# A two-layer FFN kernel on one core: the second layer's transposes move from TensorE to VectorE

## The reference

```python
def _L1_cond_ref(x, c, weight, c_weight, bias):
    out = lax.conv_general_dilated(x, weight, window_strides=(1,), padding=[(4, 4)],
                                   dimension_numbers=('NCH', 'OIH', 'NCH'), feature_group_count=4)
    return out + (c @ c_weight.T)[:, :, None] + bias[None, :, None]

def _L1_ffn_ref(x, up, down, perm):            # H = 16 heads, d = 128, m = 512
    t = x.reshape(-1, 2048)[:, perm].reshape(-1, 16, 128)
    t = gelu(einsum('bhd,hdm->bhm', t, up), approximate=False)
    t = einsum('bhm,hmd->bhd', t, down).reshape(-1, 2048)
    return t[:, argsort(perm)]
x = x + _L1_ffn_ref(_L1_cond_ref(x, cond_128, ...), up, down, perm)
```

## Time and profile before

| | |
|---|---|
| time, median of 3 runs | 2580.77 us (2577.89 to 2582.27) |
| the profiled execution's own time | 2583.87 us |
| its span (first to last instruction) | 2582.0 us |
| TensorE busy | 2528.0 us, 98% |
| VectorE busy | 1822.8 us, 71% |
| ScalarE busy | 1001.8 us, 39% |
| GpSimd busy | 950.8 us, 37% |
| moved by DMA | 541.02 MB, mean 210 GB/s |
| mean granted TensorE clock | 0.996 of 2.4 GHz |

### The profile page before, as it was taken

One profiled execution on the slowest core, in us unless ns is written; L12 is line 12 of the kernel. 1 busy time (PEld: TensorE's weight loads), 2 busy tenths in 40 slices (PEclk: granted clock), 3 DMA queues, 4 the chain that ended last, 5 costly groups with the idle time before them and its releaser, 6 DMA issues.

```text
span 2582.0 us, 39106 instructions
## 1 busy us (share of the span) xinstructions
PE 2528.0 (98%) x12090; PEld 2099.3 (81%) x12090; DVE 1822.8 (71%) x2667; ACT 1001.8 (39%) x1632; POOL 950.8 (37%) x826
## 2 busy tenths in 40 slices
PE   8899999999999999999999999999999999999997
PEld 6788888888888888888888778888888888888775
DVE  6665555965556755576445768888888888888876
ACT  3221212321122322232222555555555555555573
POOL 2366645466654455233223212222222222222231
PEclk9999999999999999999999999999999999999998
DMA  9965644665545777576555754577767676777786
GB/s 318 322 196 199 201 168 155 238 210 197 196 163 185 228 229 228 161 250 210 160 165 186 223 153 131 170 219 219 221 214 226 205 223 205 225 226 223 212 281 240
DMA packets 417281, 541.02 MB, mean 210 GB/s; under 512 B 36248, under 2 KB 270064, under 8 KB 417072
## 3 DMA queue, kind: packets, MB, share of 16 engines
q1 hardware_dynamic: 314816, 307.40, 39.6%
q10 hardware_dynamic: 78144, 154.27, 15.9%
q0 software_dynamic: 24112, 76.80, 9.4%
HBM read 309.72 MB, written 228.61 MB: 208 GB/s over the span
## 4 chain that ended last, share of the span: by engine, by line
PE 91%; DVE 4%; DMA 2%; issue 2%; ACT 1%; ACTq 0%; SPq 0%; POOL 0%; DVEq 0%; POOLq 0%
PE ps_c L461 44%; PE ps_up L1398 13%; PE ps_y L1408 13%; PE ps_c L1423 9%; PE ps_v L439 4%; PE ps_c L427 2%; PE ps_zt L1436 2%; PE ps_f L1444 2%; DVE w_lo L1004 1%; PE ps_up L1423 1%; DVE ring_lo L951 0%; DVE r_early L1000 0%; DMA a_s<-in_lora_a 0%; DMA x_n<-in_up 0%; DMA aggw_d<-agg 0%
## 5 line engine op out<-in xcount | busy, mean ns | idle before, releaser
L461 PE MATMUL ps_c<-w_hi,ring_hi 128*128 128x512 f32 x1792 | 703.8, 393 | 3.8 <-DVE r_early L1000 3.2
L461 PE MATMUL ps_c<-w_hi,ring_lo 128*128 128x512 f32 x1792 | 698.0, 390 | 0.0
L461 PE MATMUL ps_c<-w_lo,ring_hi 128*128 128x512 f32 x1792 | 697.8, 389 | 0.0
L611 ACT ACTIVATE ring_hi<-raw_n 128x512 fp32r<-128x512 f32 x382 | 239.4, 631 | 848.7 <-DVE raw_n L942 235.1
L1380 POOL DMA_INDIRECT y_d<-y_s,idx x128 | 145.7, 1139 | 723.1 <-ACT y_s L1548 689.6
L1505 ACT ACTIVATE kern<-ps_up 128x512 f32<-128x512 f32 x512 | 306.6, 599 | 257.5 <-PE ps_up L1398 245.4
L461 PEld LDWEIGHTS ps_c<-w_hi,ring_hi 128*128 128x128 f32 x1792 | 336.7, 188 | 74.5 <-issue 4.0
L461 PEld LDWEIGHTS ps_c<-w_hi,ring_lo 128*128 128x128 f32 x1792 | 336.4, 188 | 70.2
L461 PEld LDWEIGHTS ps_c<-w_lo,ring_hi 128*128 128x128 f32 x1792 | 336.7, 188 | 67.3
L1622 DVE TENSOR_TENSOR g_lo<-kern,g_hi 128x512 fp32r<-128x512 f32 x512 | 354.5, 692 | 38.2 <-ACT g_hi L1509 21.8
L1000 DVE TENSOR_TENSOR r_early<-ps_c,r_early 128x512 f32<-128x512 f32 x256 | 176.6, 690 | 276.2 <-PE ps_c L461 276.2
(11 more groups left out here) (211 smaller groups left out, 3832.9 us busy)
## 6 DMA issues: line engine op xcount, KB each, us to landing
u_d<-raw_n ACTq DMA_DIRECT2D x64, 512.0 KB, 3.2
x_d<-r_early ACTq DMA_DIRECT2D x128, 256.0 KB, 3.6
raw_n<-u_d SPq DMA_DIRECT2D x64, 512.0 KB, 3.6
x_d<-x_s ACTq DMA_DIRECT2D x126, 256.0 KB, 2.7
u_s<-x_d SPq DMA_DIRECT2D x496, 64.0 KB, 2.2
z_d<-x_s SPq DMA_DIRECT2D x120, 256.0 KB
rear<-y_d SPq DMA_DIRECT2D x112, 256.0 KB
rear<-x_d SPq DMA_DIRECT2D x112, 256.0 KB, 4.0
```

Source lines behind the costliest of these rows:

```text
L461: mm = nc.tensor.matmul(bank, a[:, dc, :], w[k][:, dc, :], start=(first and dc == 0 and n == 0), stop=(dc == 3 and n == 2), skip_group_che ...
L611: nc.scalar.activation(ring_hi[g % RING][:].rearrange("p a n -> p (a n)"), factor(q, k, p), ACT.Copy).then_inc(hi_ready, 1)
```

## The change

TensorE's `turn_z` and `turn_y`, with their banks `ps_zt` and `ps_f`, go. VectorE transposes 32x32 blocks inside each quarter of the partitions instead: `turn_z` from `z_s` straight into `zt` (in place of `take_z`), and, for two steps at once, `turn_y` from the loaded rows into `o_s`, followed one step later by `add_x1`, without a stride. For that the layouts change: a tile `zt` holds one group of four batches, a store of it takes one quarter of the partitions (32) with 16 pieces of 512 bytes each, rows of `y_d` come back in four DMAs of 32 partitions, the residual and the output move 512 KB for a pair of steps in 1 KB pieces, and `out` is written phase by phase and reordered on the host. There are two `z_s`, two pairs `t_hi`/`t_lo` (split two steps ahead, gathered three ahead), and two result banks `ps_y`. ScalarE makes two of four high parts of the hidden layer in all steps. A second pair of split convolution inputs for the lead steps has its own memory, and waits for layer 0's end go with that. A tile's store is issued in the step of its last convolution, no longer two steps later.

```diff
-                    sh.load_group(sp, x1_d, sh.xp[t - 4], t - 4, 0, t - 4)
+                    sh.load_group(sp, x1_d, sh.xp[t - 4], t - 4, t - 4, 0)
...
-        ps_c, ps_zt, ps_y, ps_f = bank("ps_c"), bank("ps_zt"), bank("ps_y"), bank("ps_f")
+        ps_c, ps_last = bank("ps_c"), bank("ps_last")
+        ps_y = [bank(f"ps_y{j}") for j in range(2)]
...
+        def by_scalar(mc):
+            return mc % 2 == 0
...
+        def final_part(dram, k, w):
+            first, cols = SB * (k - 1), slice(w % 2 * 2 * P, (w % 2 + 1) * 2 * P)
+            return dram[bass.ds(first, SB), :, w // 2, cols].rearrange("b c q -> c b q")
+        def z_rows(dram, r, part):
+            return dram.rearrange("(w i r) n -> r i w n", w=WIDE, r=S)[r, :, :, part * C:(part + 1) * C]
...
-            def load_final(k, h, parity):
+            def load_rows(k, h, parity):
...
-                wait(sp, fin_done, v - 1)
-                sp.dma_start(yt_s[j], y_d[1 - parity][c * 512:(c + 1) * 512, h // 4 * C:(h // 4 + 1) * C]
-                             .rearrange("(l p) r -> p l r", p=P)).then_inc(yt_in[j], 16)
-                wait(sp, o_ready, v - 1)
-                sp.dma_start(x1_s[j], x1_d[b, :, :, c * P:(c + 1) * P]).then_inc(x1_in[j], 16)
+                wait(sp, fin_done, pair(k, h))
+                rows = y_d[1 - parity].rearrange("(q w i s) n -> q s i w n", q=2, w=8, s=S)[w % 2, w // 2]
+                for g in range(G):
+                    sp.dma_start(yt_s[g * GC:(g + 1) * GC, :].rearrange("p (w n) -> p w n", w=8),
+                                 rows[:, :, g * C:(g + 1) * C]).then_inc(yt_in, 16)
+            def load_final_x1(k, h):
+                wait(sp, o_out, 16 * pair(k, h))
+                sp.dma_start(x1_s.rearrange("p (b q) -> p b q", b=SB), final_part(x1_d, k, h // 2)).then_inc(x1_in, 16)
...
+                for r in range(2 if isinstance(u, int) and u == H - 1 else S):
+                    sp.dma_start(z_rows(z_d[(parity + ahead) % 2], r, jb),
+                                 zt_of(k, h)[r * GC:(r + 1) * GC].rearrange("p w b c -> p w (b c)")).then_inc(z_out[jb % 2], 16)
...   (SyncE's step)
+                if h % 2 == 0 and pair_exists(k, h):
+                    load_rows(k, h, parity)
+                if h % 2 == 1 and pair_exists(k, h):
+                    load_final_x1(k, h)
+                if exists(k, h, LEAD) and (h + LEAD) % G == G - 1:
+                    store_z(k, h, parity)
+                if h % 2 == 0 and pair_exists(k, h, 1):
+                    store_out(*before(k, h, 2))
...   (TensorE)
-                if exists(k, h, LEAD - 1):
-                    turn_z(*before(k, h))
-                if final_exists(k, h, 1):
-                    turn_y(*before(k, h))
...
-                    wait(pe, y_ready, s)
+                    wait(pe, y_ready, s - 1)
...   (ScalarE)
-                    wait(act, zt_done, u - 1 if paired(k, h) else u)
+                    wait(act, zt_ready, u - 1)
+                    nc.scalar.activation(z_s[h % 2][:], conv_bank(k, h), ACT.Identity,
...   (VectorE)
+            def turn_z(k, h):
+                dve.wait_ge(z_ready, u + 1)
...
+                nc.vector.transpose(zt_of(k, h)[:, :, n % SB, :], z_s[h % 2][:]
+                                    .rearrange("p (w c) -> p w c", w=WIDE)).then_inc(zt_ready, 1)
+            def turn_y(k, h):
+                dve.wait_ge(yt_in, 64 * (pair(k, h) + 1))
+                nc.vector.transpose(o_s.rearrange("p (b w i) -> p b w i", b=SB, w=8),
+                                    yt_s.rearrange("p (w b c) -> p b w c", w=8, b=SB)).then_inc(fin_done, 1)
+            def add_x1(k, h):
+                dve.wait_ge(fin_done, pair(k, h) + 1)
+                dve.wait_ge(x1_in, 16 * (pair(k, h) + 1))
+                nc.vector.tensor_tensor(x1_s, o_s, x1_s, ALU.add).then_inc(o_ready, 1)
...   (VectorE's step: split_t two ahead, then)
+                if exists(k, h, LEAD):
+                    turn_z(k, h)
+                if not lead(k) and exists(k, h, LEAD + 1):
+                    split_x(*after(k, h))
+                if h % 2 == 1 and pair_exists(k, h):
+                    turn_y(k, h)
+                if h % 2 == 0 and pair_exists(k, h, 1):
+                    add_x1(*before(k, h, 2))
```

More of the change, by code:

```diff
@@ L1146, in drive, with store_last @@
             step(BLOCKS, 0, 0)
-            step(BLOCKS, 1, 0)
         last_yt, last_x1 = [fp32(w_hi[c][:]) for c in range(4)], [fp32(w_lo[c][:]) for c in range(4)]
         last_sum = ([sh.x1_s[:].rearrange("p a n -> p (a n)")[:, n * 512:(n + 1) * 512] for n in range(4)]
-                    + [xp[j][:, 0:512] for j in range(2)] + [z_s[:]] + t_s + [g_s[:, mc, :] for mc in range(MC)]
-                    + [x1.rearrange("p s q -> p (s q)") for x1 in x1_s] + o_s[:1])
-        last_ps = [ps_f[:, 0, :], ps_c[:, 0, :], ps_zt[:, 0, :], ps_up[:, 0, :]]
+                    + [xp[j][:, 0:512] for j in range(2)] + [z[:] for z in z_s] + t_s + [g_s[:, mc, :] for mc in range(MC)]
+                    + [rear[:, j, :] for j in range(2)])
+        last_ps = [ps_last[:, 0, :], ps_c[:, 0, :], ps_up[:, 0, :], ps_up[:, 1, :]]
         def last_unit(v):
-            return NB - SB + v % 4, v // 4
+            return v % 4, v // 4
+        def store_last(eng, v, batches):
+            g, c = last_unit(v)
+            eng.wait_ge(last_o, v + 1)
+            for b in batches:
+                eng.dma_start(out[NB - SB + b, g * GC:(g + 1) * GC, c, :], last_sum[v][b * GC:(b + 1) * GC, :]).then_inc(last_o_out, 16)
         def lead(k):
@@ L1308, in step @@
                     load_x1(*after(*after(k, h)))
-                if exists(k, h, LEAD - 2) and (h + LEAD - 2) % G == G - 1:
-                    store_z(k, h, parity)
-                if not lead(k) and exists(k, h, LEAD + 2):
+                elif not lead(k) and exists(k, h, LEAD + 2):
                     load_x1(*after(*after(k, h)))
@@ L1425, in conv @@
                 mm.then_inc(conv_done, 1)
-            def turn_z(k, h):
-                u, _, _, _ = conv_unit(k, h)
-                z = z_pair[pair_of(k, h)]
-                if isinstance(k, int) and u == 0:
-                    pe.wait_ge(small_in, 32)
-                    pe.wait_ge(sh.u_read[1], 4 * QUADS)
-                pe.wait_ge(z_ready, u + 1)
-                wait(pe, zt_ready, u)
-                for w in range(4):
-                    mm = nc.tensor.transpose(ps_zt[:, 0, w * P:(w + 1) * P], z[:, w * P:(w + 1) * P], id_s[:])
-                mm.then_inc(zt_done, 1)
-            def turn_y(k, h):
-                v, j, _, _ = final_unit(k, h)
-                pe.wait_ge(yt_in[j], 16 * (H // 2 * (k - 1) + h // 2 + 1))
-                wait(pe, o_ready, v)
-                for l in range(4):
-                    mm = nc.tensor.transpose(ps_f[:, 0, l * P:(l + 1) * P], yt_s[j][:, l, :], id_s[:])
-                mm.then_inc(fin_done, 1)
             def step(k, h, parity):
@@ L1505, in gelu @@
                 nc.scalar.activation(g_s[:, mc, :], ps_up[:, mc, :], ACT.Gelu).then_inc(gelu_done, 1)
-                if by_scalar(k, h, mc):
+                if by_scalar(mc):
                     act.wait_ge(gelu_done, MC * s + mc + 1)
-                    act.wait_ge(down_done, MC * (s - 1) + mc + 1)
+                    wait(act, down_done, MC * (s - 1) + mc + 1)
                     nc.scalar.activation(g_hi[:, mc, :], g_s[:, mc, :], ACT.Copy).then_inc(ghi_scalar, 1)
             def step(k, h, parity):
-                if not lead(k) and exists(k, h, 1) and not early(*after(k, h)):
-                    split_t(*after(k, h))
+                if not lead(k) and exists(k, h, 2):
+                    split_t(*after(*after(k, h)))
                 if lead(k):
```

237 lines of the change are left out of this document (86 added, 151 removed).

## The result

The kernel after takes **2507.3 us** (median of 4 runs, 2506.1 to 2513.5), the kernel before 2580.0 on the same chip: a ratio of 0.972, 95% interval 0.971 to 0.974. The forecast was 2484, with a range of 2460 to 2550. So the sign and the range hold, and 23 of the 97 us forecast are missing.

A forecast was written before the change was run, and what follows sets the result against it. TensorE was taken as the bound, so its removed transposes are gained: -80 - 8 - 5 - 4 = -97 us from 2583.87 gives 2487, and the runs' median, 3.1 lower, 2484; range 2460 to 2550.

The forecast's parts named there:

- Rival A: Tile stores, layer 1: VectorE waits for stores to land; if landing takes 12 us, 27 tiles stall, +46, 2530; chance 0.13.
- rival C: VectorE, layer 1: transposes near twice a copy fill 7.4 of 7.55 us, waits paid in full; +50, 2535; chance 0.11.
- Steps 0 to 107: Layer 1 with convolutions: TensorE stays the bound without its transposes, 7.55 us a step; -8 (0 to 16) and -80 (17 to 107).
- Rival B: `turn_z` and `turn_y` on VectorE: slow transposes, twice the price still under TensorE, four times gives 2690; slower, chance 0.11.
- Step 4: Lead steps: SyncE's queue hides the removed transposes, but loads begin sooner and `z_d` completes earlier; -4 us, from 0 to -8.
- Step 3: Steps 108 to 126, no convolution: matmuls alone allow -17 us, transfers and a new loop stand against it; -5 us taken.
- the loop of `x1_s`: Late stage: one buffer added in place, stored, reloaded; 10.4 to 13.0 us per two steps, binding at the upper end.
- the floor of 5.47: Steps 108 to 126: matmuls alone, 24 x 0.228 = 5.47 us a step, against 6.37 before.
- Step 5: The end: 16 last adds lose their stride, but each result costs two DMA issues, 0.92 us together; 0, from -5 to +5.

## Why the prediction was right, and where it failed

The large term, 88 of the 97 us, came out for the reason given. The small ones did not: in the profiled execution 12.8 us are missing in the lead, 7.3 in the late stage and 1.7 at the end, all on one side, so nothing cancelled. The range held them because its room above the forecast had been left for rivals A and C, which did not come.

- **Steps 0 to 107**: -87.4 us measured, -88 forecast. The matmul pitches were the step: 7.55 forecast, 7.57 measured. VectorE was busy 586.18/91 = 6.44 us a step (6.4 forecast), ScalarE 5.77 (6.0). Rival B falls with the transposes' 711 and 1234 ns, rival C with TensorE's waits, which are under 1 us in all of steps 17 to 107.
- **Rival A** did not come, but its mechanism is there. VectorE waited for a tile up to 1.4 us: stores landed up to 6.9 + 1.4 = 8.3 us after the turn, short of the 10.3 from which it was to cost. The statement in B that transposes of twice the price would leave VectorE under TensorE is true of its work and wrong for the time: with only the turns of z doubled, 7.07 us of work, the stage lost 16.7 us. Rival C has this mechanism, waits paid in full by a full VectorE, but priced it for a VectorE of 7.4 us; A and B were priced one by one, though VectorE's slack and the cover of the stores are the same microsecond.
- **Step 4, the lead** (-4 forecast, +8.8 measured) is the largest miss. I said that SyncE's queue binds, and then counted as a gain that `z_d` is complete earlier, without pricing the move that brings it: a store in its own step waits for the turn, and the next units' input loads stand behind. I also took a tile's stores at the 2.60 us of 128-partition DMAs, where they took 3.39, and every load at 0.46, where the two behind a store took 2.98 together. The sum of 9.9 us for four units was short even of the kernel before: from one tile's store to the next it takes 11.6 us (1474.55 to 1486.17), and 15.1 in the kernel after. Moving the stores back gave 6 to 7 us, wide stores 10.
- **Step 3, the late stage** (-5 forecast, bounds +2 to -17; +2.3 measured). The load that I named, a DMA share of 0.92, was there (0.91), but as a mean over the stage. The 4 MB of the last residual go out in four bursts, as before, but the change had put them onto 32 partitions, and the prediction did not mention them. Without them the stage takes 106.8 us, -14, near the floor; they cost 16.6. My one mechanism, the loop of `x1_s`, doesn't bind in the kernel after. The second bank, counted in the floor of 5.47 but with no price of its own, is worth 5 to 7.5 us of the stage.
- **Step 5, the end** (0 forecast, +1.7): the two sides were right, an addition every 0.6 to 0.85 us and then the queue, with 32 issues on SyncE in 17.7 us (0.55 each and not 0.46). Merging 12 of them shortened the issuing by 4.0 us, started it 2.5 later, and gave back 1.0 us in all, near what repeats of this stretch differ by (35.8 to 36.7). Whether the issues or the bytes set its length stays open.

## What to carry to other kernels

Where an engine's slack hides both its own work and a wait for a transfer, price them together: each fits, and the sum does not. When a store moves up in a queue, ask what it waits for and what stands behind it. And read the DMA share of a stage by its bursts: once the steps get shorter, a megabyte issued at once ahead of a gather costs idle time and then clock. The position of a DMA in a queue has a price beyond its own: the two loads behind a tile's store took 2.98 us where two others take 0.9.

## What the runs showed of the hardware

- 32x32 transposes of fp32 on VectorE: 711 ns over 128x512, 1234 ns over 128x1024, within 4% of an addition there (687 and 1216 ns), though one side is read or written with a stride between blocks.
- A DMA whose outermost dimension is 4 on the DRAM side ran on about a quarter of the engines and held up what was queued behind it, 35.5 us over the stage against the same bytes with 128.
- DMAs over 32 partitions: 0.04 more DMA share in steps 17 to 107 than over 128, for z stores and row loads alike (with another order of the pieces in DRAM). Stores so shaped also slow the issuing queue, 0.85 us a store against 0.58, and the two loads behind four of them took 2.98 us together against 1.36; other loads start about every 0.46 us.
- TensorE at the lower clock after a wait of 3.30 us: a pitch of 0.43 us in place of 0.23.
